# A chunked linear-attention layer and its low-rank mixture on eight cores: first norm split over two engines, V products moved, second norm's sums rewritten

## The reference, cut to what matters

```python
x = layernorm(x + attention(x))      # projections q, k, v, s, g; running state; out product Wo
h = relu(x @ W1 + b1)                # [rows, 2048]
alpha = softmax(h @ W2 + b2)         # [rows, 8]
vx = einsum('krd,bsd->bskr', V, x)   # 8 experts of rank 64: 512 columns
out = einsum('bsk,bskd->bsd', alpha, einsum('kdr,bskr->bskd', U, vx))
x = layernorm(x + out)               # (x - mean) / sqrt(var + eps), output in f32
```

## Time and profile before

| | us |
|---|---|
| median of 3 runs | 924.24 (922.14 to 924.28) |
| the profiled execution, its time | 924.83 |
| its span on the slowest core (core 2) | 923.3 |
| spans of the even cores | 919.9 to 923.3 |
| spans of the odd cores | 884.2 to 888.9 |
| PE busy | 864.8 (94% of the span) |
| DVE busy | 375.1 (41%) |
| ACT busy | 354.1 (38%) |
| POOL busy | 137.6 (15%) |
| store of 512 KB of y, issue to landing, median | 2.7 |
| load of 1 MB of W1, issue to landing, median | 12.8 |

### The profile page before, as it was taken

The page is one execution under the profiler, slowest core; times in us unless marked ns, Lnnn a source line. Parts: engine busy times, 40 slices in busy tenths (PEclk is TensorE's granted clock), DMA queues, the critical chain, the costliest instruction groups (busy, mean ns, idle before and its releaser), DMA issues.

```text
span 923.3 us, 15483 instructions; the slowest of 8 cores (884.2 to 923.3 us)
## 1 busy us (share of the span) xinstructions
PE 864.8 (94%) x5729; PEld 464.9 (50%) x5729; DVE 375.1 (41%) x876; ACT 354.1 (38%) x745; POOL 137.6 (15%) x183
## 2 busy tenths in 40 slices
PE   3999999999999999999999999999989999999972
PEld 2444554555555555555555554444445666655531
DVE  2332044545445454454544555464543000012254
ACT  0111244655555555565555554102233222213343
POOL 4000011221122211222112222001000000001223
PEclk9999999999999999999999999999999999999997
DMA  8999602123511244111640027938507700031224
GB/s 135 166 171 171 126 1 44 29 38 75 92 30 33 38 86 92 23 34 39 137 93 1 17 83 177 256 109 152 122 1 141 122 13 1 1 68 44 94 116 187
DMA packets 13187, 77.49 MB, mean 84 GB/s; under 512 B 1712, under 2 KB 1712, under 8 KB 5936
## 3 DMA queue, kind: packets, MB, share of 16 engines
q0 software_dynamic: 8928, 57.51, 34.7%
q1 hardware_dynamic: 4176, 18.90, 5.3%
HBM read 124.47 MB, written 9.44 MB: 145 GB/s over the span
## 4 chain that ended last, share of the span: by engine, by line
PE 83%; DVE 6%; ACT 5%; issue 4%; DMA 1%; DVEq 0%; POOL 0%; POOLq 0%; ACTq 0%
PE p L225 58%; PE no L225 16%; PE tb L225 5%; PE aw L225 2%; ACT scrb_a L269 2%; PE st L225 1%; DVE x_a L245 1%; DMA xst_a<-x_main 1%; DVE bst_a L1015 1%; DVE xfm_a L257 1%; ACT kq_a L275 1%; ACT gt_a L269 1%; ACT mv_a L269 0%; DVE okb_a L245 0%; DVE ms_a L260 0%
## 5 line engine op out<-in xcount | busy, mean ns | idle before, releaser
L225 PE MATMUL p<-s_a,xfm_a 128*128 128x512 bf16 x1152 | 260.4, 379 | 8.9 <-ACT kq_a L275 8.9
L225 PEld LDWEIGHTS p<-s_a,xfm_a 128*128 128x128 bf16 x1152 | 110.5, 98 | 135.2 <-issue 12.5
L566 POOL TENSOR_TENSOR ng_a<-ng_a,gt_a 128x512 f32<-128x512 f32 x36 | 45.7, 1269 | 308.1 <-ACT gt_a L269 255.3
L245 DVE TENSOR_TENSOR awm_a<-aw,cbs 128x1024 bf16<-128x1024 f32 (+1 forms) x38 | 44.4, 1168 | 111.9 <-PE aw L225 111.9
L225 PE MATMUL p<-x2fm_a,s_a 128*128 128x384 bf16 x512 | 87.4, 326 | 0.0
L225 PE MATMUL p<-s_a,ofm_a 128*128 128x512 bf16 x352 | 79.6, 379 | 1.8 <-DVE x_a L245 1.8
L225 PE MATMUL p<-xfm_a,wq_a 128*128 128x384 bf16 x384 | 66.2, 326 | 0.0
L225 PE MATMUL p<-xfm_a,wk_a 128*128 128x384 bf16 x384 | 64.4, 326 | 0.0
L225 PEld LDWEIGHTS p<-x2fm_a,s_a 128*128 128x128 bf16 x512 | 48.3, 97 | 31.7 <-issue 0.6
L225 PEld LDWEIGHTS p<-s_a,ofm_a 128*128 128x128 bf16 x352 | 33.8, 98 | 40.0 <-issue 1.9
L225 PE MATMUL no<-s_a,ofm_a 128*128 128x512 bf16 x224 | 51.0, 379 | 0.0
(11 more groups left out here) (146 smaller groups left out, 1127.2 us busy)
## 6 DMA issues: line engine op xcount, KB each, us to landing
s_a<-w1p POOLq DMA_DIRECT2D x10, 1024.0 KB, 12.8
x_a<-x_main SPq DMA_DIRECT2D x9, 1024.0 KB, 11.1
s_a<-wvp POOLq DMA_DIRECT2D x8, 1024.0 KB, 13.0
s_a<-wgp POOLq DMA_DIRECT2D x8, 1024.0 KB, 12.7
s_a<-wop POOLq DMA_DIRECT2D x8, 1024.0 KB, 13.0
y<-x_a SPq DMA_DIRECT2D x16, 512.0 KB, 2.7
xst_a<-x_main POOLq DMA_DIRECT2D x9, 512.0 KB, 27.9
wq_a<-wqp POOLq DMA_DIRECT2D x4, 1024.0 KB, 8.0
```

The source lines that it names most:

```text
L225: return t.matmul(out, lhsT, rhs, start=start, stop=stop, is_transpose=tp, skip_group_check=skip)
L245: return vop(lambda v: v.tensor_tensor(out, a, b, op), waits)
L566: g_tok[it] = gop(lambda e: e.tensor_tensor(b, b, gt.ap(0, 512), ALU.mult), [sg, n])
```

## The change

Three things. In `ln1` the normalised block is written in two halves: columns 0 to 1023 by GpSimd from mean and `rst1` (subtract, multiply), columns 1024 to 2047 by ACT with scale and bias; each half has its own token, and each group of eight transposes waits for its own half. A second bias `nbs`, smaller by the root of 2048, is made for the squares. The V products of the second group leave the place before the W1 loop and stand behind it, with two banks, the last two first-group pairs between them; the transposes of the softmax stand behind the third. The W1 panel 0 is loaded again into the place of panel 1, when the unit with et = 7 has run. The pairs of the first group are spread differently: 10 of 12 within the loop. In `ln2` the squares are scaled so that their sum is a mean square, the variance is made by four small DVE operations, the last of the sums being added in ACT's Ln, and the norm is (x - mean) * r without a bias. The last chunk's last pair is taken in two halves of 512 columns, and its norm is split over DVE (1216 columns) and GpSimd (832). The buffers of sums are now released by GpSimd's second norm operation and not by DVE's bias.

```diff
@@ -1008,7 +1010,7 @@
 
 
     x2_tok, ln_tok, bn_tok = {}, {}, {}
-    xb_mm = [None]
+    xb_mm = [None, None]
     ot_end = of_tok[last]
 
     def ln_part(c, n, tok):
...
@@ -1020,17 +1022,21 @@
         t = vop(lambda v: v.bn_aggr(m.ap(0, 2), bst[c].ap(0, 24)), [bn_tok[(c, n)] for n in range(4)])
         l = s_act(m.ap(2, 1), m.ap(1, 1), AF.Ln, bias=eps_ap, waits=[t])
         r = s_act(rst1.ap(c, 1), m.ap(2, 1), AF.Exp, scale=-0.5, waits=[l])
-        nb = v_ts(m.ap(3, 1), m.ap(0, 1), rst1.ap(c, 1), -1.0, ALU.mult, ALU.mult, [r])
-        ln_tok[c] = s_act(scrb.ap(0, D), x1[c].ap(0, D), AF.Identity, bias=m.ap(3, 1),
-                          scale=rst1.ap(c, 1), waits=[nb, xb_mm[0], ot_end])
+        nb = v_ts(nb1.ap(c, 1), m.ap(0, 1), rst1.ap(c, 1), -1.0, ALU.mult, ALU.mult, [r])
+        v_ts(nbs.ap(c, 1), m.ap(0, 1), rst1.ap(c, 1), -1.0 / D ** 0.5, ALU.mult, ALU.mult)
+        g0 = gop(lambda e: e.tensor_scalar(scrb.ap(0, D // 2), x1[c].ap(0, D // 2), m.ap(0, 1), rst1.ap(c, 1),
+                                           ALU.subtract, ALU.mult), [t, r, xb_mm[0], ot_end])
+        g1 = s_act(scrb.ap(D // 2, D // 2), x1[c].ap(D // 2, D // 2), AF.Identity, bias=nb1.ap(c, 1),
+                   scale=rst1.ap(c, 1), waits=[nb, xb_mm[1], ot_end])
+        ln_tok[c] = (g0, g1)
 
     def x2_transposes(c, half):
         tok = None
         for j in range(8):
             k = half * 8 + j
             tok = mm(TB[:, j * 128:(j + 1) * 128], scrb.ap(k * 128, 128), ident, True, True,
-                     [ln_tok[c], tb_free[0]] if j == 0 else [], inc=(j == 7), tp=True)
-        xb_mm[0] = tok
+                     [ln_tok[c][half], tb_free[0]] if j == 0 else [], inc=(j == 7), tp=True)
+        xb_mm[half] = tok
         ev = v_copy(x2fm.ap3(half * 8 * TM + c * 128, [[TM, 8], [1, 128]]), TB[:, :],
                     [tok] + [wo_done[(c, n)][0] for n in range(4)])
         tb_free[0] = ev
...
@@ -1084,7 +1090,8 @@
         b = h_n[0] % 3
         h_n[0] += 1
         pn, j = divmod(et, 4)
-        m = unit(bank[:, 0:w], bank, lambda k: w1[pn].ap(k * 512 + j * 128, 128),
+        wt = w1[1] if grp and pn == 0 else w1[pn]
+        m = unit(bank[:, 0:w], bank, lambda k: wt.ap(k * 512 + j * 128, 128),
                  lambda k: x2fm.ap(k * TM + t0, w), KC, [x2_tok[cc] for cc in chunks_of([t])], ktok)
         ev = s_act(hT[b].ap(0, w), bank[:, 0:w], AF.Relu, bias=cfs.ap(8 + et, 1),
                    waits=[m, al_mm[-3] if len(al_mm) >= 3 else None, ot_end])
...
@@ -1133,12 +1140,12 @@
 
     vx_tok, ae_tok = {}, {}
 
-    def vx_unit(t, j):
+    def vx_unit(t, j, banks):
         t0, w = t
-        bank = next_bank(gen)
+        bank = next_bank(banks)
         m = unit(bank[:, 0:w], bank, lambda k: v2.ap(k * KR + j * 128, 128), lambda k: x2fm.ap(k * TM + t0, w),
                  KC, [x2_tok[cc] for cc in chunks_of([t])], t_v2)
-        ev = s_copy(vx[j].ap(t0, w), bank[:, 0:w], [m, ot_end, xb_mm[0]])
+        ev = s_copy(vx[j].ap(t0, w), bank[:, 0:w], [m, ot_end, *xb_mm])
         set_free(bank, ev)
         vx_tok[(t0, j)] = ev
         return m
...
@@ -1159,59 +1166,69 @@
     turn = [0]
     s_used = {}
     sums = {}
-    sq_done = [ln_tok[NM - 1]]
-
-    def u_pair(c, h2, npair):
-
+    sq_done = [ln_tok[NM - 1][1]]
+
+    def u_part(c, i, lo, n, acc, waits):
+
+
+        b = c % 3
+        xs = x1[c].ap(lo, n)
+        t = vop(lambda v: v.scalar_tensor_tensor(xs, xs, rst1.ap(c, 1), acc, ALU.mult, ALU.add,
+                                                 accum_out=us[b].ap(i, 1)),
+                waits + [*ln_tok[c]] + s_used.get(b, []))
+        sq_done[0] = s_sum(sqd.ap(0, n), xs, AF.Square, nbs.ap(c, 1), 1.0 / D ** 0.5, uq[b].ap(i, 1),
+                           [t, sq_done[0]] + s_used.get(b, []))
+        sums[(c, i)] = (t, sq_done[0])
+        return t
+
+    def u_bank(c, n, bank):
+        return unit(bank[:, :], bank, lambda k: vx[k].ap(c * 128, 128), lambda k: ut.ap(k * D + n * 512, 512),
+                    4, [t_ut], lambda k: ae_tok[(c, k)])
+
+    def u_pair(c, h2, npair, split=False):
 
         two, parts = pairs[turn[0] % npair]
         turn[0] += 1
-        for i, bank in enumerate(parts):
-            n = 2 * h2 + i
-            m = unit(bank[:, :], bank, lambda k: vx[k].ap(c * 128, 128), lambda k: ut.ap(k * D + n * 512, 512),
-                     4, [t_ut], lambda k: ae_tok[(c, k)])
-        xs = x1[c].ap(h2 * 1024, 1024)
-        b = c % 3
-        t = vop(lambda v: v.scalar_tensor_tensor(xs, xs, rst1.ap(c, 1), two[:, 0:1024], ALU.mult, ALU.add,
-                                                 accum_out=us[b].ap(h2, 1)),
-                [m, ln_tok[c]] + s_used.get(b, []))
-        for bank in parts:
-            set_free(bank, t)
-        sq_done[0] = s_sum(sqd.ap(0, 1024), xs, AF.Square, mv[c].ap(3, 1), uq[b].ap(h2, 1),
-                           [t, sq_done[0]] + s_used.get(b, []))
-        sums[(c, h2)] = (t, sq_done[0])
+        ms = [u_bank(c, 2 * h2 + i, bank) for i, bank in enumerate(parts)]
+        if split:
+            for i, bank in enumerate(parts):
+                u_part(c, 1 + i, 1024 + 512 * i, 512, bank[:, :], [ms[i]])
+        else:
+            t = u_part(c, h2, h2 * 1024, 1024, two[:, 0:1024], [ms[1]])
+            for bank in parts:
+                set_free(bank, t)
 
     def ln2(c, split):
+
         b = c % 3
         m, u, q = mv[c], us[b], uq[b]
         (a0, q0), (a1, q1) = sums[(c, 0)], sums[(c, 1)]
-        t0 = v_tt(u.ap(2, 1), u.ap(0, 1), u.ap(1, 1), ALU.add, [a0, a1])
-        t1 = v_ts(u.ap(3, 1), u.ap(2, 1), 1.0 / D, m.ap(3, 1), ALU.mult, ALU.add, [t0])
-        t2 = v_tt(u.ap(3, 1), u.ap(3, 1), u.ap(3, 1), ALU.mult, [t1])
-        t3 = v_tt(q.ap(2, 1), q.ap(0, 1), q.ap(1, 1), ALU.add, [q0, q1])
-        t4 = v_stt(q.ap(3, 1), q.ap(2, 1), 1.0 / D, u.ap(3, 1), ALU.mult, ALU.subtract, [t2, t3])
-        l = s_act(m.ap(2, 1), q.ap(3, 1), AF.Ln, bias=eps_ap, waits=[t4])
-        r = s_act(m.ap(2, 1), m.ap(2, 1), AF.Exp, scale=-0.5, waits=[l])
-        nb = v_ts(m.ap(1, 1), u.ap(2, 1), -1.0 / D, m.ap(2, 1), ALU.mult, ALU.mult, [r])
-        s_used[b] = [nb, l]
+        e0 = v_ts1(q.ap(4, 1), q.ap(0, 1), eps_ap, ALU.add, [q0])
+        s0, last_ = u.ap(0, 1), 1
+        if split:
+            a0 = v_tt(u.ap(4, 1), u.ap(0, 1), u.ap(1, 1), ALU.add, [a0, a1])
+            e0 = v_tt(q.ap(4, 1), q.ap(4, 1), q.ap(1, 1), ALU.add, [e0, q1])
+            s0, last_ = u.ap(4, 1), 2
+            a1, q1 = sums[(c, 2)]
+        mu = v_ts(u.ap(5, 1), s0, u.ap(last_, 1), 1.0 / D, ALU.add, ALU.mult, [a0, a1])
+        d = v_ts1(u.ap(6, 1), u.ap(5, 1), nb1.ap(c, 1), ALU.add, [mu])
+        nv = v_stt(q.ap(5, 1), u.ap(6, 1), u.ap(6, 1), q.ap(4, 1), ALU.mult, ALU.subtract, [d, e0])
+        l = s_act(m.ap(2, 1), q.ap(5, 1), AF.Ln, bias=q.ap(last_, 1), scale=-1.0, waits=[nv, q1])
+        r = s_act(m.ap(3, 1), m.ap(2, 1), AF.Exp, scale=-0.5, waits=[l])
 
         def norm(eng, lo, n, sem):
             xs = x1[c].ap(lo, n)
-            if eng == "s":
-                o = s_act(xs, xs, AF.Identity, bias=m.ap(1, 1), scale=m.ap(2, 1), waits=[nb])
-            elif eng == "v":
-                o = v_ts(xs, xs, m.ap(2, 1), m.ap(1, 1), ALU.mult, ALU.add, [nb, r])
-            else:
-                o = gop(lambda e: e.tensor_scalar(xs, xs, m.ap(2, 1), m.ap(1, 1), ALU.mult, ALU.add), [nb, r])
+            o = (vop if eng == "v" else gop)(
+                lambda e: e.tensor_scalar(xs, xs, u.ap(5, 1), m.ap(3, 1), ALU.subtract, ALU.mult), [mu, r])
             ydma(yout[c * 128:c * 128 + 128, lo:lo + n], xs, sem, [o])
+            return o
 
         if split:
-            norm("s", 0, 512, "OD0")
-            norm("v", 512, 768, "OD1")
-            norm("g", 1280, 768, "OD2")
+            norm("v", 0, 1216, "OD0")
+            norm("g", 1216, 832, "OD1")
         else:
             norm("g", 0, 1024, "OD0")
-            norm("g", 1024, 1024, "OD1")
+            s_used[b] = [norm("g", 1024, 1024, "OD1"), l]
 
 
     units = [(et, t) for et in range(KC) for t in first_g]
...
@@ -1226,58 +1243,61 @@
             al_unit(i == 1, False)
         if et == 3 and t is first_g[-1]:
             t_v2 = halves(v2, KR, sh.v2p, 0, f"R{HSLOT[0]}", [m])
-    all_t = [(t, j) for t in role.tiles for j in range(4)]
-    for i, (t, j) in enumerate(all_t):
-        m = vx_unit(t, j)
+    for i, (t, j) in enumerate([(t, j) for t in first_g for j in range(4)]):
+        vx_unit(t, j, gen)
         if i == 0:
             al_unit(False, True)
             at1 = alpha(first_g)
-        if i == 4:
+        if i == 3:
             at1 = alpha_T(first_g, at1)
-    w1_again = halves(w1[0], 512, sh.w1p, 0, f"R{HSLOT[0]}", [m])
 
 
     muls = [(t, j) for t in first_g for j in range(4)]
     todo = [("u", c, h2) for c in chunks_of(first_g) for h2 in range(2)]
     order = list(range(4, KC)) + list(range(4))
     t = second_g[0]
-    hold, n_u = 4, len(todo)
+    n_u = len(todo)
     behind = []
 
```

(37 more changed lines are left out.)

12 lines of the change are left out of this document (7 added, 5 removed).

## The result

The changed kernel takes 944.38 us (median of 4 runs, 941.36 to 944.82), the kernel before, beside it on the same chip, 924.26 us. The ratio is 1.0212, with an interval of 1.0191 to 1.0234: 2.1% slower, where 1.8% faster was forecast, and far above the range.

What follows compares the result with a forecast made beforehand. PE was taken as the bound, its matmuls 83% of the chain, with gains in the first norm and after 880 us: 923.3 - 8.3 - 8.0 = 907.0; + 1.5 - 0.6 = 908 us (-1.8%), range 903.5 to 913.5.

Steps and rivals of the forecast that it cites:

- part 1: First norm split between POOL and ACT: PE's 1.03 us wait a period goes, POOL's half taking 1.19 us; -8.3 us.
- rival (a): First norm: POOL's half is slow and PE waits for it eight times; at 4.8 us the kernel takes 935.7; chance 0.03.
- part 4: Kernel's end: last two-operand sums wait for POOL's norm, DVE's and POOL's last norms run one behind the other; -8.0 us.
- Part 2: V products moved behind the W1 loop cover waits before the second group's U pairs; first scaled sum starts 6.2 us earlier.
- full clock at T: T, the last V product's end, was put at 886.9 us; PE was expected at full clock there, 1.3 us gained.
- rival (c): The clock falls at the last V product's end, as it did at 894: +1.3 us, so 909.3; chance 0.2.
- Part 3: Second norm after the W1 loop: DVE needs 3.3 us a chunk, below PE's 3.46, so PE sets the tail.
- rival (b): DVE's two-operand sums at the end hardly wait, slipping in between POOL's two operations: 905.3 us; chance 0.17.

Runs made afterwards that it cites:

- experiment 1: Changed kernel with GpSimd's half of the first norm as multiply-add, the second norm left subtract-multiply: 921.13 us, ratio 0.9972 to the kernel before.
- experiment 2: Changed kernel with the second norm as multiply-add with a bias again, the first norm's half left subtract-multiply: 933.20 us, ratio 1.0115 to the kernel before.
- experiment 4: Changed kernel with subtract-multiply kept, but both scalars of the second norm in one tile: 941.5 us (one run).
- experiment 5: Kernel before plus ten GpSimd operations with nothing beside them, results unused: at 1024 columns multiply-add took 1.2 us, subtract-multiply 3.8 us.
- experiment 6: Changed kernel with both norms as add-multiply, (x + (-mean)) * r, without a bias on GpSimd: 906.48 us, ratio 0.9816 to the kernel before.
- experiment 3: Changed kernel with both norms as multiply-add with a bias: 912.22 us, ratio 0.9874 to the kernel before.
- experiment 7: experiment 6 with V products, W1 reload and first-group pairs placed as in the kernel before: 912.33 us, ratio 0.9878 to the kernel before.
- experiment 8: experiment 6 with ACT writing the whole first-norm block, as in the kernel before: 916.78 us, ratio 0.9922 to the kernel before.
- experiment 9: experiment 6 with two of the second group's four alpha products ahead of the last V product, on four banks: 906.37 us, ratio 0.9811 to the kernel before.
- experiment 11: Kernel before plus unused single-source operations on DVE, then POOL; only durations read: DVE 0.80 to 0.82 us for each of four pairs at 1024 columns.
- experiment 10: Kernel before plus six GpSimd operations, DVE two-operand products beside three, then a 768-column DVE multiply-add: one product took 1.01 us beside either form, the 768 columns 0.67.

## Why the prediction was wrong, and where it was right

**The step that failed** is the price in part 1: "I take 1.19 (same size, same operation)". It was not the same operation. L1205 multiplies and adds; the new code subtracts and multiplies, and on POOL that pair takes 3.78 us, 3.2 times as long (experiments 1, 2, 4, 5). Size and type, at which the step looked, were not what set it (1194 ns into f32, 1196 into bf16 with multiply-add). The bound of 4.8 us held the value, but rival (a) had 0.03 for it, and for the wrong reason (bf16). Its mechanism and formula were right: at 3.78 us the block is ready for PE at 643.85 + 3.78 + 0.25 = 647.88, which is 646.45 + 1.43; measured was +1.45 a period.

**The same oversight in ln2** carried the old price on without a word: part 4 lets POOL norm chunk 7 "from 902.3 to 904.6", two operations at 1.19, and takes 0.90 for its last 832 columns. The edit from multiply-add to subtract-multiply was read as one that takes a bias away, on DVE. But its 16 operations on POOL grew from 1.19 to 3.81 us, 42 us in all. Under the W1 loop this is hidden; after it, three chunks' norms of some 7.6 us and the last of 3.1 stand one behind the other, and D to end takes 20.4 us instead of 11.5. Experiment 2 takes out just this and gets 11.7. With both orders mended (experiment 6) the kernel is at 906.5 us, so these two prices, with the waits and the low clock that came with them, account for the whole miss. The low clock wasn't in the forecast: in the norm stage, between 640 and 712 us, it shows on cores 0 and 4 of the changed kernel and on core 6 of experiment 4, and on no even core of the kernel before or of experiments 1, 3, 6, 7, 8 and 9, where POOL's half is fast or absent. Experiment 2 has the slow half and shows none, so the wait doesn't always bring it.

**Part 1, apart from the price:** forecast -8.3 us, period 7.8. Experiment 6 against 8: 8.3 us in that stage, 7.9 against the kernel before; period 7.80. Right.

**Part 2, the V move:** forecast -6.2 us to the first scaled sum, of which 1.3 from the clock. Experiment 6 against 7: 5.9 us in the medians. The changed kernel itself shows -4.8 in B to C; the forecast's first U pair starts at about 889.0 (its end less 1.89), so -5.1 was forecast. The sum is right, the split partly luck: against experiment 7 only 3.6 us are earlier work and 2.4 are clock, since on core 0 two pairs were slow, where core 2, from which the forecast was read, had one. The forecast's full clock at T failed in the changed kernel: rival (c), the clock falling at the first pair, is what cores 0 and 4 show (2.77 and 3.04 us, and 2.60 and 2.98, for the first two pairs), while cores 2 and 6 kept full clock. In experiment 6 only core 6 shows it, with 3.53 us for that pair and 14.2 from C to D.

**Part 3, the second norm:** forecast 3.46 us a chunk, set by PE. Measured 3.6 and 3.4 in experiment 6, 4.72 with the bias back in (experiment 3). Right, once POOL is fast; in the changed kernel DVE waited 3.16 us for POOL instead. Part 3 never costed what it means that POOL's norm now gives back the sum buffers.

**Part 4, the end:** forecast that the two-operand sums wait for POOL's norm, and that DVE's and POOL's last norms run one behind the other, 0.91 + 0.90. Experiment 6 shows 0.91 for DVE, and POOL, begun at 895.82, ending at 897.49, 0.83 behind DVE. Of the last chunk's three two-operand sums the first waited 0.8 us, until the first of POOL's two operations ended (893.73); the second slipped in before the next operation took hold; the third, the variance, waited 0.2 us for the end of that one. So the truth lies between the forecast, in which all wait to the end, and rival (b), whose argument was that no sum waits into the first of two. D to end is 12.1 us where 908.1 + 7.2 - 902.3 = 13.0 was forecast.

All parts of the sum but the price of POOL's operation stand within about 1 us. The chance given to slower, 0.03, rested on an argument about a row that wasn't read to its end: the row names the class of the instruction, TENSOR_SCALAR, and not its operations; these stand only in the source line.

## What to carry to other kernels

A row's price belongs to the operation pair in the source, not to the name of its class: when a change reorders an elementwise pair on POOL, treat it as an operation without a price. Write an affine step on POOL as multiply-add or add-multiply: here (x + (-mean)) * r instead of (x - mean) * r took 66 us off POOL's busy time (60.8 + 34.0 + 3.1 down to 19.0 + 10.8 + 1.7) and turned +2.1% into -1.8%. And when a buffer's release moves to another engine, that engine's queue becomes part of the chain.

## What the runs showed of the hardware

- POOL on 1024 f32 columns: 1.2 us for multiply-add, add-multiply, multiply-multiply; 3.8 us for each of the other five pairs tried; 2.85 us for a single add, subtract or multiply. The Trainium skill (GPSIMD Engine Reference, Engine selection) calls one-input work on it roughly line-rate. The first group comes nearest to that, at 1.2 us against DVE's 0.8 (four pairs measured); the other pairs are at less than a quarter of DVE's rate. Why these pairs are fast wasn't looked into.
- POOL shuts a two-operand DVE operation out for the first 1.2 us, whether its own takes 1.2 or 3.8 us. The Trainium skill (SBUF — State Buffer, two separate sides) says that the loser is blocked for the whole instruction. The fast form can't tell the two apart; the slow form does, and measurement decides: in these rows it was blocked for the first 1.2 of the 3.8 us, and two-operand operations begun 1.2 to 3.1 us into it ran at their usual length.
- One thing stays open: DVE's norm of 1216 columns took 1.61 us in the changed kernel, beside POOL's slow form, and 0.91 in experiment 6. DVE's form isn't the reason (experiment 11). It begins 2.8 us into one slow POOL operation and ends 0.66 us into the next, and that one, begun at 926.35, takes 4.30 us instead of 3.78:

```profile
922.57 8.09 POOL L1222 TENSOR_SCALAR x_a<-x_a,us_a,mv_a 128x1024 f32<-128x1024 f32 x2
```

  Both took longer than alone, though at 0.91 us DVE's would have ended at 926.31, before the next one began; what holds them isn't shown. The same start within POOL's operation, and the same 1.61 or 1.62 us, stand on all eight cores of the changed kernel and of experiments 1 and 4, so no run varies it; the 768 columns of experiment 10 lay within one POOL operation.
